# A Mamba block and a mixture-of-experts layer on one core: residual sums, layer-norm sums and Newton steps moved between engines

## The chip, the cores and the metric

One core of one Trainium2 chip. The time is the device time of one execution in microseconds (us); it is the median of three runs. The core has five engines that run their own instruction queues in order and meet through semaphores: TensorE (PE), VectorE (DVE), ScalarE (ACT), GpSimd (POOL) and SyncE (SP), which issues the transfers. A difference below about 0.2% can't be told from no change.

## The reference, cut to what matters

The input is 4 sequences of 2048 tokens with 256 features. With a state-space layer of 512 inner channels and 16 states, and a router that picks 2 of 4 experts (a shared matrix and a rank-4 addition for each):

```
x  = x + ssm(layernorm(x))
       u = W_in LN(x) + b_in -> x_i (512), z (512)
       dt, B, C = W_x x_i + b_x ;  delta = softplus(W_dt dt + b_dt)
       h_t = h_(t-1) * exp(delta_t A) + x_t * delta_t * B_t ;  y_t = sum over states of h_t C_t
       out = W_out ((y + D x_i) * silu(z)) + b_out
x  = x + moe(layernorm(x))
       logits = W_g LN(x) + b_g ; top 2 of softmax -> w
       out = sum over the 2 experts of w * W_o relu(W_i LN(x) + B_e A_e LN(x))
layernorm(x) = (x - mean) / sqrt(var + 1e-5)
```

## The kernel before, in words

**Tiles.** The 8192 tokens are cut into 16 chunks of 512. A chunk is 4 tiles of 128 tokens by 256 features where tokens lie on partitions (`xin`, `xr`, `x1`, 0.5 MB each), and tiles of 128 channels by 512 tokens where channels do. The scan works on 512 channels x 16 states = 64 units of 128 rows (32 channels x 4 states) by 512 tokens.

**Main loop.** A chunk has 16 steps (`s`), a step 4 units (`j`). For each step GpSimd multiplies delta*x by B for all four units into `hs` (L1344, `times_b`, one step ahead). For each unit ScalarE writes exp(delta A) into a PSUM bank, `decay` (L1089), and VectorE scans it with `hs` (L1286). Then the result is multiplied by C: the first two units of a step always by VectorE (L1276), the last two by GpSimd in 12 of the 16 steps (L1356, `POOL_STEPS`), by VectorE in the others. TensorE sums the products over the states into `y_ps` (L946). ScalarE keeps the last column of the scan as the next chunk's state (L1103, `keep_state`), and only then writes the next `decay` into the same bank.

**Side jobs.** All else is cut into jobs of a letter and a number, and tables of rows (`PE_SIDE`, `ACT_SIDE`, `DVE_SIDE`, `POOL_SIDE`, `SP_SIDE`) say at which step and which quarter of it an engine runs which job: a row is a step, `|` separates the four quarters (two for TensorE). "pre" is work for the next chunk, "main" for this one, "post" for the one before, "late" for the one before that. The jobs run in each engine's queue behind the scan work of that quarter. `LAST` and `END` are tables of their own for the last chunk and the tail after it. The jobs that matter here:
- N (`stats`): sums of the first layer norm on VectorE, `bn_stats` for 4 tiles (N0), `bn_aggr` for 4 (N1). P0 and P1 the same for the second norm.
- A1/A2 of POOL (`center`, L663 to L666): variance + eps, minus the mean, minus half the variance. R (L1039, L1041): 1/sqrt by Ln and Exp on ScalarE. O1/O2 of POOL (`newton`, L673 to L682): one Newton step on it, five instructions of 128x4. O and Q of ACT (L1047): the normalising itself.
- A, G: transposes; B, E: W_in; C: W_x, copied by ScalarE twice (L1001, L1002; the second rounds to fp32r), then VectorE subtracts it to keep the rest (L1167, `dt_st` of 64 rows). D: W_dt. L, M, U, V: softplus.
- Y of PE and F: W_out, whose result VectorE adds to `xr` (L1187, the first residual). H, I, X, M: the router. J, S, T: the experts' hidden layer; K: W_o, 8 products of 256 columns (L932), whose result VectorE adds to `x1` (L1190, the second residual). SyncE stores `x1`.
- W of POOL (L1330), a 128x4 product of the router's weights.

PSUM has eight banks: four of `decay`, one of `y_ps`, and three that the jobs share in the order of the PE table (`assign_banks`); a bank is free when the engine that evacuates it is done (`freed_at`).

Semaphores count finished instructions. `xin` of the next chunk is loaded when A1 has read it, `xr` when G1 has read it (step 11).

## Time and profile before

| | |
|---|---|
| median of 3 runs | 1964.43 us (1963.17 to 1964.9) |
| the profiled execution | 1968.13 us, of which the span 1966.3 us |
| busy share of the span | PE 83%, VectorE 93%, ScalarE 73%, GpSimd 91% |
| instructions | PE 6816, VectorE 2246, ScalarE 2755, GpSimd 780 |
| transfers | 234.92 MB, mean 119 GB/s |
| granted TensorE clock, mean | 0.933 of full |

The span runs from the first to the last instruction of the profile. Busy time is the time in which an engine had at least one instruction under way; records of neighbours overlap a little. A groups row has the line, the engine, the operation, output<-input with shapes and count, then the busy time and the mean ns of one, then the time in which the engine stood idle just before such an instruction and who ended it. GpSimd and VectorE are the busiest; the share of a whole span mixes prologue, 14 alike chunks and a tail.

### The profile page before, as it was taken

Reading aid. Unit: us, or ns where it says so; the run is one execution under the profiler, and the core shown is the slowest. Engines: PE = TensorE matmul, PEld = TensorE weight load, DVE = VectorE, ACT = ScalarE, POOL = GpSimd, SP = SyncE. Lnnn points to the kernel's source line nnn. Section 1 sums busy time; section 2 is a strip of 40 time slices with the busy share of each in tenths; the row PEclk is TensorE's granted clock in tenths of the full one; section 3 lists DMA queues with packets and bytes.
Section 4 is the critical chain, followed back from the end, with each engine's and each line's share of the span. In section 5 each row is a group of like instructions: output and inputs, shape, how many; then the busy total and the mean of one; then the engine's idle time right before and its main releaser. Section 6 shows DMA issues by size and latency. Waiting matters only on the chain.

```text
span 1966.3 us, 25727 instructions
## 1 busy us (share of the span) xinstructions
PE 1628.6 (83%) x6816; PEld 808.6 (41%) x6816; DVE 1823.1 (93%) x2246; ACT 1431.6 (73%) x2755; POOL 1791.7 (91%) x780
## 2 busy tenths in 40 slices
PE   3364779898898989889898988889898898988899
PEld 1111224444443444444344444444444444444456
DVE  2799999999999999999999999999999999999951
ACT  3566767877787777878777787877778787777643
POOL 1899999999999999999999999999999999999920
PEclk8666879999899999989999999999999999999999
DMA  4646553544646365464636536463643646265200
GB/s 167 142 112 155 119 138 90 142 123 92 161 111 155 91 152 123 96 151 112 161 84 149 126 92 152 112 165 79 158 118 94 148 111 166 68 156 118 58 14 19
DMA packets 146761, 234.92 MB, mean 119 GB/s; under 512 B 22064, under 2 KB 46896, under 8 KB 146096
## 3 DMA queue, kind: packets, MB, share of 16 engines
q1 hardware_dynamic: 146608, 233.18, 48.7%
q8 instruction: 59, 0.97, 0.2%
q14 instruction: 94, 0.77, 0.1%
HBM read 190.11 MB, written 42.99 MB: 119 GB/s over the span
## 4 chain that ended last, share of the span: by engine, by line
DVE 32%; POOL 23%; issue 17%; PE 17%; ACT 5%; DMA 1%; DVEq 0%; SPq 0%; POOLq 0%; ACTq 0%
POOL hs L1344 14%; DVE decay L1286 13%; DVE hs L1276 8%; DVE hs L1286 7%; POOL hs L1356 6%; PE bank L910 4%; PE bank L932 4%; ACT decay L1089 2%; PE y_ps L946 2%; POOL e_dt L1334 1%; DVE st L1146 1%; POOL z_dt L1323 1%; PE bank L894 1%; PE bank L914 1%; PE bank L884 1%
## 5 line engine op out<-in xcount | busy, mean ns | idle before, releaser
L1344 POOL TENSOR_TENSOR hs<-dx_rep,b_rep 128x2048 f32<-128x2048 f32 x256 | 1161.8, 4541 | 13.4 <-issue 11.1
L1286 DVE TENSOR_TENSOR_SCAN decay<-decay,state,hs 128x512 f32<-128x512 f32 x640 | 796.2, 1277 | 34.2 <-ACT decay L1089 27.4
L1089 ACT ACTIVATE decay<-dt_rep,a_sb 128x512 f32<-128x512 f32 x1024 | 690.0, 685 | 28.7 <-DMA dt_rep<-rep_scratch 10.3
L1286 DVE TENSOR_TENSOR_SCAN hs<-decay,state,hs 128x512 f32<-128x512 f32 x384 | 487.3, 1269 | 4.3 <-ACT decay L1089 3.7
L1356 POOL TENSOR_TENSOR hs<-hs,c_rep 128x1024 f32<-128x1024 f32 x192 | 453.6, 2362 | 6.3 <-ACT state L1103 6.3
L1276 DVE TENSOR_TENSOR hs<-decay,c_rep 128x1024 f32<-128x1024 f32 x320 | 385.1, 1204 | 0.0
L946 PE MATMUL y_ps<-hs,nsum 128*32 128x512 f32 x2048 | 290.3, 641 | 48.8 <-POOL hs L1356 30.6
L910 PE MATMUL bank<-w_i_sb,x_t 128*128 128x512 f32 x484 | 273.5, 693 | 28.9 <-DVE silu L1174 25.5
L868 PE MATMUL bank<-xn_t,w_in_sb 128*128 128x512 f32 x512 | 258.5, 635 | 14.5 <-ACT x_t L996 4.9
L1103 ACT COPY state<-decay 128x2 f32<-128x2 f32 x320 | 51.0, 159 | 266.8 <-DVE hs L1276 260.1
L932 PE MATMUL bank<-w_o_sb,r_t 128*128 128x256 f32 x944 | 224.1, 392 | 2.6 <-ACT r_t L1074 1.8
L932 PEld LDWEIGHTS bank<-w_o_sb,r_t 128*128 128x128 f32 x944 | 182.0, 195 | 50.4 <-ACT r_t L1074 15.7
L868 PEld LDWEIGHTS bank<-xn_t,w_in_sb 128*128 128x128 f32 x512 | 92.4, 197 | 141.4 <-issue 94.2
L910 PEld LDWEIGHTS bank<-w_i_sb,x_t 128*128 128x128 f32 x484 | 92.7, 209 | 136.0 <-issue 94.3
L927 PE MATMUL bank<-ident,r 128*128 128x128 f32 x928 | 123.4, 276 | 21.5 <-DVE x L1190 19.0
L927 PEld LDWEIGHTS bank<-ident,r 128*128 128x128 f32 x928 | 102.9, 140 | 61.5 <-DVE x L1190 30.2
L884 PE MATMUL bank<-w_out_sb,gated 128*128 128x256 f32 x496 | 121.1, 386 | 7.6 <-DVE x L1187 5.2
L1065 ACT ACTIVATE r<-bank,wgt 128x512 f32<-128x512 f32 x121 | 82.1, 679 | 45.3 <-PE bank L914 41.3
L884 PEld LDWEIGHTS bank<-w_out_sb,gated 128*128 128x128 f32 x496 | 90.3, 190 | 50.8 <-DVE x L1187 17.8
L946 PEld LDWEIGHTS y_ps<-hs,nsum 128*32 128x32 f32 x2048 | 42.2, 111 | 154.3 <-issue 139.6
L1069 ACT ACTIVATE r<-bank,wgt 128x512 f32<-128x512 f32 x121 | 81.9, 677 | 28.4 <-PE bank L839 28.2
L1334 POOL TENSOR_TENSOR e_dt<-e_dt,z_dt 128x1024 f32<-128x1024 f32 x32 | 75.5, 2358 | 27.6 <-ACT e_dt L1016 27.6
(163 smaller groups left out, 1747.7 us busy)
## 6 DMA issues: line engine op xcount, KB each, us to landing
dx_rep<-rep_scratch SPq DMA_DIRECT2D x256, 256.0 KB, 4.7
dt_rep<-rep_scratch SPq DMA_DIRECT2D x256, 256.0 KB, 7.6
b_rep<-bc_scratch SPq DMA_DIRECT2D x256, 64.0 KB, 3.9
rep_scratch<-z_dt SPq DMA_DIRECT2D x64, 256.0 KB, 2.5
rep_scratch<-e_dt SPq DMA_DIRECT2D x64, 256.0 KB, 2.7
c_rep<-bc_scratch SPq DMA_DIRECT2D x256, 64.0 KB, 2.6
xin<-in_u SPq DMA_DIRECT2D x16, 512.0 KB, 4.2
xr<-in_u SPq DMA_DIRECT2D x16, 512.0 KB, 4.3
```

Source lines behind the costliest of these rows:

```text
L868: mm = pe.matmul(ps[:], w_in_sb[:, k, col:col + P], xn_t[odd][:, k, :], start=k == 0, stop=k == KD - 1)
L884: pe.matmul(ps[:, cols], gated[odd][:, k, i * P:(i + 1) * P], w_out_sb[:, k, :], start=k == 0 and not (is_last(q) and i % 2), stop=False, ...
L910: pe.matmul(ps[:], x2_t[odd][:, k, t * P:(t + 1) * P], w_i_sb[:, k, cols], start=k == 0, stop=False, skip_group_check=is_last(q))
L927: mm = pe.matmul(ps[:, f * P:(f + 1) * P], r[i % 2][:, f * P:(f + 1) * P], ident[:], start=r is r1, stop=r is r2, is_transpose=True)
L932: mm = pe.matmul(ps[:, 0:D], r_t[:, f, :], w_o_sb[:, f, :], start=f == 0, stop=f == NF - 1)
L946: mm = pe.matmul(y_ps[32 * j:32 * j + 32, :], nsum[:], hs[s % 4][:, j, :], start=k == 0, stop=k == KG - 1, skip_group_check=True)
L1089: nc.scalar.activation(decay[:, j, :], dt_rep[m % 2][:, j, :], ACT.Exp, scale=a_sb[:, J * s + j:J * s + j + 1]).then_inc(decay_ready, 1)
L1276: v.tensor_tensor(hs[s % 4][:, js, :], decay[:, js, :], c_rep[:, k, :].unsqueeze(1).to_broadcast([P, 2, T]), ALU.mult).then_inc(prod_vecto ...
L1286: v.tensor_tensor_scan(hs[s % 4][:, j, :] if kept else decay[:, j, :], decay[:, j, :], hs[s % 4][:, j, :], state[:, b, n:n + 1], ALU.mult, ...
L1334: g.tensor_tensor(e_dt[:], e_dt[:], z_dt[:], ALU.add).then_inc(delta_ready, 1)
L1344: nc.gpsimd.tensor_tensor(hs[s % 4][:], dx_rep[m % 2][:], b_rep[:, k, :].unsqueeze(1).to_broadcast([P, J, T]), ALU.mult).then_inc(input_re ...
L1356: nc.gpsimd.tensor_tensor(hs[s % 4][:, 2:4, :], hs[s % 4][:, 2:4, :], c_rep[:, k, :].unsqueeze(1).to_broadcast([P, 2, T]), ALU.mult).then_ ...
```

## The change

The first residual: TensorE starts each F with a product identity x `xr`, and ScalarE copies the sum to `x1` with the row sums of its accumulator. The second residual: TensorE starts each K with identity x `x1`, ScalarE copies. The last chunk keeps VectorE's additions. The sums of both norms: ScalarE takes the row sums of x (N0, N1; or with the F copies), the mean (N2, P0), and the row sums of (x - mean)^2 by Square with the accumulator (N3, N4, P1, P2). The first chunk's first norm and the last chunk's second one keep `bn_stats` on VectorE (`FIRST`, `by_vector`). ScalarE also computes minus half the variance and the square of the root, so that Newton is three instructions, and these and the centering go to VectorE (O1 in step 1, O2 in step 7). The rest of dt: TensorE adds -identity x `dt_st` to C0's bank, ScalarE copies it (C1). The C product of step 14's last two units goes from GpSimd to VectorE. The tables have a new order of jobs.

```diff
 ACT_SIDE = [
+    "N0 pre, N1 pre | N2 pre | N3 pre | N4 pre, S1 late",
+    "R1 pre | J2 late | J3 late | T1 late, O0 pre, O1 pre, O2 pre",
...
+    "S4 late | E1 main | J5 late, V1 main, R2 post, W1 main, Z1 main | ",
+    "Q0 post | Q1 post, C0 pre | K1 late, C1 pre | D0 pre",
...
 DVE_SIDE = [
-    "N0 pre, N1 pre |  |  | ",
-    " |  |  | Y3 post",
...
+    "O1 pre |  |  | Y3 post",
...
+    " |  | O2 post, S1 main | ",
...
 POOL_SIDE = [
-    "A1 pre, O1 pre",
+    "",
...
-    "A2 post",
-    "O2 post",
+    "",
+    "",
...
-POOL_STEPS = [s for s in range(STEPS) if s % KG < 3]
+POOL_STEPS = [s for s in range(STEPS) if s % KG < 3 and s != 14]
...
+FIRST = dict(SIDE, act=[[[x for x in part if x[0] != "N"] for part in row] for row in SIDE["act"]],
+             dve=[[["N0 pre", "N1 pre", "A1 pre", "O1 pre"]] + [[]] * (J - 1)] +
+             [[[x for x in part if x != "O1 pre"] for part in row] for row in SIDE["dve"][1:]])
...
+        def newton(dve, i, q):
+
+            v = nc.vector
...
+            dve.wait_ge(halved, q + 1)
+            dve.wait_ge(root, 3 * (q + 1))
+            v.tensor_tensor(nw[:, 1], nw[:, 0], nw[:, 3], ALU.mult).then_inc(steps, 1)
+            dve.wait_ge(steps, NEWTON_STEPS * q + 1)
+            v.scalar_tensor_tensor(out=rs[:], in0=nw[:, 1], scalar=1.5, in1=rs[:], op0=ALU.add, op1=ALU.mult).then_inc(steps, 1)
+            dve.wait_ge(steps, NEWTON_STEPS * q + 2)
+            v.tensor_tensor(nt[:], nw[:, 4], rs[:], ALU.mult).then_inc(steps, 1)
...
+                if letter == "C" and i == 1:
...
+                    pe.wait_ge(dt_hi, q + 1)
+                    pe.matmul(banks[used("C0", c, AHEAD[when])[0]][:], neg_id[:], dt_st[:], start=False, stop=True,
+                              skip_group_check=True).then_inc(dt_rest, 1)
+                    return
...
                 elif letter in "YF":
...
+                    if not is_last(q):
+                        if i == 0:
+                            pe.wait_ge(xr_loaded, 16 * (q + 1))
+                        pe.matmul(ps[:, cols], ident[:], xr[:, i, :], start=True, stop=False)
...
                 elif letter == "K":
+                    if not is_last(q):
+                        needs("F", i)
+                        pe.matmul(ps[:, 0:D], ident[:], x1[odd][:, i, :], start=True, stop=False)
...
+                elif letter == "N":
+                    if i == 0:
+                        act.wait_ge(xin_loaded, 16 * (q + 1))
+                    if i < 2:
+                        for t in (2 * i, 2 * i + 1):
+                            last = nc.scalar.activation(xin[:, t, :], xin[:, t, :], ACT.Identity, accum_out=sum1[:, t:t + 1])
+                        last.then_inc(ln1_sum, 1)
+                    elif i == 2:
+                        act.wait_ge(ln1_sum, 2 * q)
+                        nc.scalar.mul(nw1[:, 4], sum1[:], -1.0 / D).then_inc(ln1_mean, 1)
+                    else:
+                        if i == 3:
+                            act.wait_ge(ln1_mean, q)
+                        for t in (2 * i - 6, 2 * i - 5):
+                            last = nc.scalar.activation(xn_t[odd][:, t // 2, t % 2 * D:t % 2 * D + D], xin[:, t, :], ACT.Square, bias=nw1[:, 4, t:t + 1],
+                                                        accum_out=sq1[:, t:t + 1])
+                        last.then_inc(ln1_var, 1)
+                elif letter == "F":
+
+                    at_least(act, out_stored[i], 16 * (q - 1))
+                    ps, free = wait_filled(act, job[:2], c, when)
+                    nc.scalar.activation(x1[odd][:, i, :], ps[:, 0:D], ACT.Identity, accum_out=sum2[:, i:i + 1]).then_inc(free, 1)
...
+                elif letter == "K":
+                    ps, free = wait_filled(act, job[:2], c, when)
+                    nc.scalar.copy(x1[odd][:, i, :], ps[:, 0:D]).then_inc(free, 1)
...
                 elif letter == "R":
...
+                        nc.scalar.activation(nw[:, 3], sq[:], ACT.Identity, scale=-0.5 / D,
+                                             bias=consts[:, 4, 0:1]).then_inc(halved, 1)
+                        nc.scalar.activation(rs[:], sq[:], ACT.Ln, scale=1.0 / D, bias=consts[:, 0, 0:1]).then_inc(root, 1)
...
                     nc.scalar.activation(rs[:], rs[:], ACT.Exp, scale=-0.5).then_inc(root, 1)
+                    act.wait_ge(root, 3 * q + 2)
+                    nc.scalar.activation(nw[:, 0], rs[:], ACT.Square).then_inc(root, 1)
```

## Rows read from the trace of the kernel before

**Rows 1.** Busy time in one stretch: columns PE, PEld, DVE, ACT, POOL, granted clock, DMA.

```profile
200.00:1800.00 1600.00, 1385.11 (x5866) 685.95 (x5865) 1575.24 (x1919) 1239.57 (x2388) 1567.17 (x679) 0.95 0.52 124
```

**Rows 2.** Groups of VectorE instructions, 200 to 1800 us: busy, mean ns, idle before.

```profile
L1286 DVE TENSOR_TENSOR_SCAN decay<-decay,state,hs 128x512 f32<-128x512 f32 x559 | 695.8, 1277 | 8.5 <-ACT decay L1089 5.1 <-POOL hs L1344 0.6 <-issue 0.2
L1286 DVE TENSOR_TENSOR_SCAN hs<-decay,state,hs 128x512 f32<-128x512 f32 x336 | 426.5, 1269 | 4.2 <-ACT decay L1089 3.7
L1276 DVE TENSOR_TENSOR hs<-decay,c_rep 128x1024 f32<-128x1024 f32 x280 | 337.0, 1204 | 0.0
...
L1190 DVE TENSOR_TENSOR x<-bank,x 128x256 f32<-128x256 f32 x53 | 22.0, 416 | 6.4 <-PE bank L932 6.4
...
L1146 DVE BATCH_NORM_STATS2 st<-xin 128x6 f32<-128x256 f32 x52 | 18.1, 412 | 0.0
L1167 DVE SCALAR_TENSOR_TENSOR dt_st<-bank,b_x_sb,dt_st 64x512 fp32r<-64x512 f32 x14 | 10.6, 757 | 0.5
L1151 DVE BATCH_NORM_AGGREGATE mv<-st 128x2 f32<-128x6 f32 x108 | 10.2, 158 | 2.4 <-DVE st L1146 2.4
```

**Rows 3.** Timeline of GpSimd within one chunk: start us, us, instruction, idle before.

```profile
744.72 0.24 POOL L663 TENSOR_TENSOR ve<-mv,consts 128x4 f32<-128x4 f32 x1
...
747.29 4.55 POOL L1344 TENSOR_TENSOR hs<-dx_rep,b_rep 128x2048 f32<-128x2048 f32 x1
751.80 2.37 POOL L1356 TENSOR_TENSOR hs<-hs,c_rep 128x1024 f32<-128x1024 f32 x1
754.11 4.56 POOL L1344 TENSOR_TENSOR hs<-dx_rep,b_rep 128x2048 f32<-128x2048 f32 x1
...
790.50 0.20 POOL L663 TENSOR_TENSOR ve<-mv,consts 128x4 f32<-128x4 f32 x1
...
790.96 4.54 POOL L1344 TENSOR_TENSOR hs<-dx_rep,b_rep 128x2048 f32<-128x2048 f32 x1
...
797.79 0.19 POOL L673 TENSOR_TENSOR nw<-rs 128x4 f32<-128x4 f32 x1
...
799.05 4.54 POOL L1344 TENSOR_TENSOR hs<-dx_rep,b_rep 128x2048 f32<-128x2048 f32 x1
```

**Rows 4.** The same groups view for GpSimd, 200 to 1800 us.

```profile
L673 POOL TENSOR_TENSOR nw<-rs 128x4 f32<-128x4 f32 x27 | 5.4, 201 | 20.6 <-ACT rs L1041 20.6
```

**Rows 5.** Timeline of VectorE: a product; the last chunk's Newton steps.

```profile
757.64 1.20 DVE L1276 TENSOR_TENSOR hs<-decay,c_rep 128x1024 f32<-128x1024 f32 x1
758.75 1.27 DVE L1286 TENSOR_TENSOR_SCAN hs<-decay,state,hs 128x512 f32<-128x512 f32 x1
...
1904.76 0.16 DVE L673 TENSOR_TENSOR nw<-rs 128x4 f32<-128x4 f32 x1 [0.31 <-ACT rs L1041]
1904.96 0.16 DVE L676 TENSOR_TENSOR nw<-nw 128x4 f32<-128x4 f32 x1
```

**Rows 6.** Timeline of the prologue, VectorE and GpSimd, 9 to 14 us.

```profile
10.59 1.38 DVE L1120 TENSOR_TENSOR w_dt_st<-hs,w_dt_st 32x512 fp32r<-32x512 f32 x2
...
11.50 0.53 POOL L676 TENSOR_TENSOR nw<-nw 128x4 f32<-128x4 f32 x1
...
12.11 0.20 POOL L678 TENSOR_TENSOR nw<-nw,consts 128x4 f32<-128x4 f32 x1
```

**Rows 7.** Durations min/median/max of two lines over the whole run.

```profile
L676 POOL TENSOR_TENSOR nw<-nw x31: 198/201/531, 11.5 to 1820.9; 128x4 f32<-128x4 f32 x31
...
L1127 DVE TENSOR_SCALAR skip<-ident,d_sb x4: 274/274/306, 12.1 to 12.7; 128x128 f32<-128x128 f32 x4
```

**Rows 8.** Groups of ScalarE instructions, 200 to 1800 us.

```profile
L1074 ACT COPY r_t<-bank 128x512 f32<-128x512 f32 x107 | 61.7, 576 | 21.3 <-PE bank L927 21.3
L1103 ACT COPY state<-decay 128x2 f32<-128x2 f32 x279 | 44.5, 160 | 215.0 <-DVE hs L1276 208.5 <-issue 5.2
...
L1047 ACT ACTIVATE xr<-x,nt,rs 128x256 f32<-128x256 f32 x56 | 31.7, 589 | 2.8 <-POOL nt L682 2.8
```

**Rows 9.** Timeline of TensorE: the eight products of one K job.

```profile
823.18 3.62 PE L932 MATMUL bank<-w_o_sb,r_t 128*128 128x256 f32 x16
```

More of the change, by code:

```diff
@@ L151 @@
 PE_LAST = [
-    "T0 late, S1 late | J2 late",
-    " | T1 late, E0 main",
+    "S1 late | J2 late",
+    "T1 late | E0 main",
     "S2 late, F0 post, J3 late | K0 late",
-    "S3 late | T2 late, F1 post",
-    "F2 post | ",
-    "F3 post, T3 late, E1 main, J4 late | S4 late",
-    "K1 late, T4 late | ",
+    "S3 late | F1 post",
+    "F2 post, T2 late, F3 post | ",
+    "T3 late | J4 late, E1 main",
+    "K1 late, S4 late, T4 late | ",
     "J5 late | S5 late, T5 late",
-    "E2 main | ",
+    " | E2 main",
     "G0 post | ",
@@ L163 @@
     "J7 late | S7 late, T6 late, T7 late",
-    "K3 late | I0 post",
-    "E3 main, J0 post | S0 post, J1 post, T0 post",
-    "S1 post | T1 post, J2 post, K0 post",
+    "E3 main, K3 late, I0 post | ",
+    "J0 post | S0 post, J1 post",
+    "T0 post, S1 post | T1 post, J2 post, K0 post",
     " | S2 post",
@@ L376, in tables @@
         return LAST if c == NC - 1 else END
-    return SIDE
+    return FIRST if isinstance(c, int) and c < 0 else SIDE
 def parts_of(c):
@@ L403, in bank_jobs @@
                     name = {"Y": "F", "Z": "J"}.get(name[0], name[0]) + name[1]
-                if name[0] in BANK_JOBS:
+                if name[0] in BANK_JOBS and name != "C1":
                     yield name, when, J * s + j
@@ L410, in freed_at @@
     letter = name[0]
-    if letter in "FKC":
-        engine, by = "dve", name
+    if letter in "FK":
+        engine, by = "dve" if c == NC and when == "post" else "act", name
+    elif letter == "C":
+        engine, by = "act", "C1"
     elif letter == "E":
@@ L593, in block_program @@
         weights_ready = sem("weights_ready")
-        NEWTON_STEPS = 5
+        ln1_sum, ln1_mean, ln2_mean, dt_rest = (sem(n) for n in ("ln1_sum", "ln1_mean", "ln2_mean", "dt_rest"))
+        NEWTON_STEPS = 3
         def vector_products(c, s, h):
@@ L996, in job_act @@
                     nc.scalar.activation(x_t[odd][:, i, :], ps[:], ACT.Identity, bias=b_in_sb[:, i:i + 1]).then_inc(free, 1)
+                elif letter == "N":
[19 more added lines that the diff above has]
+                    nc.scalar.activation(x1[odd][:, i, :], ps[:, 0:D], ACT.Identity, accum_out=sum2[:, i:i + 1]).then_inc(free, 1)
+                elif letter == "P":
+                    if i == 0:
+                        wait_read(act, c, when, "F", range(TT))
+                        nc.scalar.mul(nw2[:, 4], sum2[:], -1.0 / D).then_inc(ln2_mean, 1)
+                    else:
+                        if i == 1:
+                            act.wait_ge(ln2_mean, q + 1)
+                        for t in (2 * i - 2, 2 * i - 1):
+                            last = nc.scalar.activation(xr[:, t, :], x1[odd][:, t, :], ACT.Square, bias=nw2[:, 4, t:t + 1],
+                                                        accum_out=sq2[:, t:t + 1])
+                        last.then_inc(ln2_var, 1)
+                elif letter == "K":
+                    ps, free = wait_filled(act, job[:2], c, when)
+                    nc.scalar.copy(x1[odd][:, i, :], ps[:, 0:D]).then_inc(free, 1)
+                elif letter == "C" and i == 1:
+                    act.wait_ge(dt_rest, q + 1)
+                    b, _ = used("C0", c, AHEAD[when])
+                    nc.scalar.activation(dt_st[64:128], banks[b][64:128], ACT.Identity,
+                                         bias=b_x_sb[64:128, 0:1]).then_inc(freed[b], 1)
@@ L1111, in _ @@
             v.memset(state[:], 0.0)
-            for n, value in enumerate((EPS, -0.5, 1.5, -1.0)):
+            for n, value in enumerate((EPS, -0.5, 1.5, -1.0, -0.5 * EPS)):
                 v.memset(consts[:, n], value)
@@ L1140, in split_lora, with stats @@
                 last.then_inc(weights_split, 1)
-            def stats(i, q, src, st, mv, part):
+            def stats(i, src, st, mv, part):
                 if i == 0:
@@ L1147, in stats @@
                 else:
-                    dve.wait_ge(part, 2 * q + 1)
+                    dve.wait_ge(part, 1)
                     dve.sem_inc(dve_turn, 1)
```

87 lines of the change are left out of this document (39 added, 48 removed), and 134 rows, old and new, of tables (ACT_END, ACT_LAST, ACT_SIDE, DVE_END).

## The prediction, made before the changed kernel was run

> **What bounds the kernel now.** I read the page first: its busy shares name VectorE (93%) and GpSimd (91%) together, which settles nothing between them. So next the busy time of a stretch without prologue and tail, 200 to 1800 us [rows 1]. The groups view of that stretch counts 559 + 336 = 895 scans [rows 2]; a chunk has 64, so 1600 us hold 13.98 chunks and a chunk takes 114.4 us. Per chunk VectorE is busy 1575.24/13.98 = 112.7 us, GpSimd 112.1, TensorE 99.1, ScalarE 88.7 [rows 1]. Two engines are within 2 us of the period, and they feed each other (GpSimd fills hs for the scan and multiplies what the scan leaves), so relieving one alone gives nothing. ScalarE spends 208.5 us of the stretch waiting in its state copies for VectorE's product [rows 8], 14.9 us a chunk: it is a follower with slack. VectorE waits for ScalarE's decay for only 5.1 + 3.7 us, 0.6 a chunk [rows 2].
>
> A record overlaps the next one: the product at 757.64 lasts 1.20 and the scan behind it starts 1.11 later [rows 5]. I price an instruction by that slot, its duration less 0.08 to 0.09.
>
> **The change, part by part, per chunk.**
>
> VectorE loses:
> - four F and four K additions (the F form is the K form with another operand): 8 x (0.416 - 0.085) = 2.6 [rows 2];
> - both layer norms' statistics: 8 x (0.412 - 0.085) = 2.6, and eight aggregations 8 x (0.158 - 0.08) = 0.6 with 2.4/13.98 = 0.2 of wait [rows 2], together 3.4;
> - the rest of dt, 0.757 - 0.08 = 0.7 [rows 2], which becomes a product with -identity on TensorE and a copy on ScalarE.
> It gains one more C product, 1.1 [rows 5], since step 14 leaves GpSimd, and two Newtons of three dependent instructions. The last chunk does such steps on VectorE already, one every 0.20 us [rows 5]: 2 x 3 x 0.20 = 1.2. Net 6.7 - 2.3 = 4.4 less; 112.7 becomes 108.3.
>
> GpSimd loses one C product, 754.11 - 751.80 = 2.3, the centering and Newton of the first norm with the wait for the root inside it, 747.29 - 744.72 = 2.6, and those of the second, (790.96 - 790.50) + (799.05 - 797.79) = 1.7 [rows 3]. That is 6.6, of which 20.6/13.98 = 1.5 was wait and not busy [rows 4]: its busy time goes to 112.1 - 5.1 = 107.0. It is now beside VectorE's 108.3 and slightly under it, so VectorE sets the period.
>
> ScalarE gains 20 instructions of 256 columns (N 8, F 4, P 4, K 4). The trace has none without pointer operands; a 256-column one with two of them takes 0.589 and a 512-column copy 0.576 [rows 8], so a slot of about 0.49 is the upper end and half of the copy, 0.24, the lower. I take 0.33, nearer to the copy since most have one pointer operand or none: 6.6. The second dt copy costs at most a copy's 0.5 to 0.6, the two means, two halves and two squares of 128x4 about 0.2 each (they are of the size of the state copy, 0.160 [rows 8]): 1.2. Sixteen of them also write an accumulator, which no row shows: from nothing to another small instruction of 0.2 each, so 0 to 3.2; I take 1.6. Sum 10.0 (6.5 to 15); ScalarE goes from 88.7 to 98.7. At nothing this is hidden by the 14.9 us in which it waits for VectorE; but the cover is thinner: the period shrinks too, and the exponential of a step can only be written after VectorE's product has read the bank, with one scan (1.277 - 0.085 = 1.19 [rows 2]) of room before the next one is wanted. Steps 0 (N0, N1 in the first quarter, N3, N4 and S1 behind), 1 (the root, then the Newton that VectorE waits for) and 7 (J5, V1, the root, W1, Z1 in one quarter, all ahead of the next exponential, with O2 waiting in the middle on VectorE) have about no room left. Today VectorE is idle 114.4 - 112.7 = 1.7 a chunk; I take 2.5 after, between 1.7 (nothing added) and 5 (each of the three steps late by a 1.2 us scan).
>
> TensorE gains eight fp32 products of 256 columns, the amount of one K job, 3.6 [rows 9], and the -identity product, under 1: 99.1 becomes 103.6. What waits behind it is mainly ScalarE's evacuations; its clock is at 0.95 of full in the stretch, mostly the higher level (2.4 GHz) [rows 1], and more work can't be expected to lower it. If the cover failed, each microsecond would appear as VectorE's wait for a gated or silu input; I leave it inside the 2.5.
>
> The dt chain gets longer: copy, product, copy, then D0 instead of copy, subtraction, D0. Its result is wanted by GpSimd three steps, some 20 us, later; no cost. K, written by ScalarE instead of VectorE, still precedes its store in the queue; the store's place on SP does not move, and F needs xr three steps after its load. No cost. Prologue and tail keep their statistics and their additions of the last chunk on VectorE; plus or minus 2 us.
>
> Sum: period 108.3 + 2.5 = 110.8 against 114.4, 3.6 a chunk. Fifteen chunks run these tables; the chunk before the tail has no first norm and gains about half. 15.5 x 3.6 = 56. The profiled execution took 1968.1 (span 1966.3), 3.7 above the median of 1964.4; off the median that gives 1909, for which I say 1910. Own range 1893 to 1940 (VectorE's idle time between 1.5 and 4.7).
>
> **Rival A, the other side: VectorE's Newton steps are held by GpSimd.** All three take both tensors from SBUF. In the prologue VectorE runs two such instructions from 10.59 to 11.97; GpSimd's L676 starts inside them at 11.50 and takes 0.53, to 12.03, that is until VectorE is done [rows 6], while the median of its 31 is 0.201 [rows 7]. So one engine holds the other. The reverse shows only in small: the longest of four skip instructions (0.306 against 0.274) has the 128x4 GpSimd instruction of 12.11 beside it [rows 6, 7]. In the steady stretch no two-SBUF VectorE instruction meets a long GpSimd one: the scan and the product read decay from PSUM, the statistics have one input. The Newtons would, 30 times (15 first norms, 15 second ones). If VectorE must wait for the instruction that GpSimd is in, the first step waits on average (16 x 4.54^2 + 15 x 2.36^2)/(2 x 108) = 1.9 us, the second, coming 0.20 after the first, for the whole next one, mean 3.5, and the third for up to as much, unless GpSimd has by then run out of scans: 5.4 to 8.9, say 6. Behind a held step stand the next scan and the C product in VectorE's queue, and ScalarE's state copy, the next exponential and GpSimd's product wait for those, so all of it is period: 30 x 6 = 180, time 1910 + 180 = 2090 (2060 to 2150). It decides from 56/30 = 1.9 a Newton: one single wait each (A1) already returns the whole gain, 1966. Against it: only the small case is shown, and a 128x4 instruction may slip in where a long one could not.
>
> The Trainium skill (SBUF — State Buffer, Who interferes with whom) says that a VectorE instruction with two SBUF inputs contends with a GpSimd instruction that reads SBUF, and that the one that starts first keeps the shared ports for its whole length. By that rule the time is that of rival A, not the 1910. The trace agrees for one direction with its 0.53 against 0.20 us [rows 6, 7]; no long GpSimd instruction here shows the other.
>
> **Rival B: ScalarE becomes the bound.** If the accumulator costs a good deal more than a small instruction (0.5 each, 8 a chunk), ScalarE stands at 105 plus its hand-overs, and VectorE waits 4 to 6 a chunk instead of 2.5. For it: steps 0, 1 and 7. Against: nothing in the trace has a ScalarE instruction that costs more than its columns and operands. Period 112.3 to 113.8, time 1930 to 1955, say 1945.
>
> **Chances.** Forecast 0.47, rival A 0.36, A1 0.07, B 0.10. Less than 0.2% (4 us) can't be told from no change. Faster: 0.47 + 0.06 (most of B) + 0.02 (half of A1's lower side) = 0.55; same: 0.05; slower: 0.36 + 0.04 = 0.40. The likeliest is 1910; because rival A holds a third, the range must reach into it: 1893 to 2110.
>
> **What would show it.** In the changed kernel's groups view the three Newton lines on VectorE at 0.16 each, with under 0.5 idle ahead, speak for 1910; durations of microseconds in them, or a GpSimd instruction lengthened beside them, for rival A. VectorE's wait for decay should grow from 0.6 to 1 or 2 us a chunk; if it grows to 4, B. ScalarE's accumulating 256-column instructions should start 0.25 to 0.6 apart, its waits in the state copies should fall from 14.9 to about 5, TensorE should be busy about 103 to 104 a chunk, and GpSimd should show waits of 3 a chunk where it shows none now. The forecast is wrong if VectorE's busy time per chunk is not within 1 us of 108.3, or if its idle time is above 5.

## Result and the profile after: 7% slower

The changed kernel takes 2101.9 us (median of four runs, 2097.6 to 2104.9) against 1964.2 before in the same job: ratio 1.070, 95% interval 1.0676 to 1.0723. The forecast, 1910, has the wrong sign; rival A, 2090, is 12 us off.

First the busy time of the same stretch in the changed kernel, which answers to [rows 1] (columns PE, PEld, DVE, ACT, POOL, clock):

```profile
200.00:1800.00 1600.00, 1393.20 (x5672) 723.40 (x5671) 1499.55 (x1563) 1273.36 (x2780) 1394.57 (x418) 0.91 0.48 116
```

and the groups of VectorE, which answer to [rows 2]; the last three are the steps of Newton:

```profile
L1357 DVE TENSOR_TENSOR_SCAN decay<-decay,state,hs 128x512 f32<-128x512 f32 x549 | 685.4, 1277 | 48.7 <-ACT decay L1166 47.5 <-POOL hs L1412 0.3 <-issue 0.2
L1357 DVE TENSOR_TENSOR_SCAN hs<-decay,state,hs 128x512 f32<-128x512 f32 x286 | 363.2, 1270 | 23.5 <-ACT decay L1166 23.4
...
L697 DVE TENSOR_TENSOR nt<-nw,rs 128x4 f32<-128x4 f32 x26 | 59.5, 2290 | 0.9
L695 DVE SCALAR_TENSOR_TENSOR rs<-nw,rs 128x4 f32<-128x4 f32 x26 | 31.2, 1202 | 0.9
...
L693 DVE TENSOR_TENSOR nw<-nw 128x4 f32<-128x4 f32 x26 | 4.9, 188 | 1.5 <-ACT nw L1118 0.8
```

549 + 286 = 835 scans are 13.05 chunks in 1600 us: a period of 122.6 us, where it was 114.4. Per chunk VectorE is busy 1499.55/13.05 = 114.9 us (forecast 108.3) and idle 7.7 (forecast 2.5); GpSimd is busy 106.9, ScalarE 97.6, TensorE 106.8. A last Newton step took 2.29 us on average; the same form in the last chunk of the kernel before took 0.16 [rows 5]. Three queues side by side in one chunk, changed kernel, VectorE, then GpSimd, then ScalarE:

```profile
720.25 0.16 DVE L693 TENSOR_TENSOR nw<-nw 128x4 f32<-128x4 f32 x1
720.44 2.23 DVE L695 SCALAR_TENSOR_TENSOR rs<-nw,rs 128x4 f32<-128x4 f32 x1
722.71 4.42 DVE L697 TENSOR_TENSOR nt<-nw,rs 128x4 f32<-128x4 f32 x1
727.05 0.74 DVE L1245 SCALAR_TENSOR_TENSOR silu<-bank,b_in_sb,e_gate 128x512 f32<-128x512 f32 x1
```
```profile
715.80 4.54 POOL L1412 TENSOR_TENSOR hs<-dx_rep,b_rep 128x2048 f32<-128x2048 f32 x1 [0.18 <-PE y_ps L973]
720.30 2.35 POOL L1424 TENSOR_TENSOR hs<-hs,c_rep 128x1024 f32<-128x1024 f32 x1
722.62 4.48 POOL L1412 TENSOR_TENSOR hs<-dx_rep,b_rep 128x2048 f32<-128x2048 f32 x1
```
```profile
727.16 0.60 ACT L1124 ACTIVATE xr<-x,nt,rs 128x256 f32<-128x256 f32 x1 [4.44 <-DVE nt L697]
```

The first step starts at 720.25, just before GpSimd's instruction of 720.30, and takes 0.16. The second starts 0.14 us after that instruction and ends, at 722.67, when it ends (722.65). The third ends at 727.13, with the next GpSimd instruction (727.10). Meanwhile ScalarE stands 4.44 us in the normalizing instruction for the shift nt, with the next exponentials behind it. Every chunk of the stretch has this at its second norm (6.8 to 7.6 us for the three steps). The first norm's steps, in the same chunk, fall where GpSimd stands still:

```profile
674.64 0.15 DVE L693 TENSOR_TENSOR nw<-nw 128x4 f32<-128x4 f32 x1
...
675.03 0.16 DVE L697 TENSOR_TENSOR nt<-nw,rs 128x4 f32<-128x4 f32 x1
```
```profile
664.75 9.02 POOL L1412 TENSOR_TENSOR hs<-dx_rep,b_rep 128x2048 f32<-128x2048 f32 x2
675.63 2.37 POOL L1424 TENSOR_TENSOR hs<-hs,c_rep 128x1024 f32<-128x1024 f32 x1 [1.86 <-ACT state L1180]
```

Over the whole run the three lines are busy 132.1 us in 96 instructions; at 0.16 each they would be 15.4. So VectorE is held for 117 us: 6.3 us at the second norm of each steady chunk, 7 in each of the first norms at 66 and 180 us, 12.5 in the Newton at 1943 us, none in the other first norms. That is most of the 138 us lost, but it is not yet the 192 us between forecast and result.

### The profile page after: what moved, and what is told of

Its sections match the earlier page's. It is cut to its first block, busy times and chain, and to the rows that moved or that the text cites. A ratio compares the mean times of both kernels' runs of the same rounds, so it can differ in the third digit from the quotient of the medians.

```text
span 2101.6 us, 26197 instructions
## 1 busy us (share of the span) xinstructions
PE 1745.9 (83%) x7072; PEld 903.8 (43%) x7072; DVE 1878.6 (89%) x1982; ACT 1573.4 (75%) x3403; POOL 1714.9 (82%) x516
## 4 chain that ended last, share of the span: by engine, by line
PE 45%; DVE 20%; ACT 13%; issue 12%; POOL 7%; DMA 1%; SPq 0%; DVEq 0%; ACTq 0%; POOLq 0%
DVE decay L1357 8%; PE bank L891 7%; PE bank L934 7%; PE bank L959 7%; PE y_ps L973 6%; DVE hs L1347 5%; POOL hs L1412 5%; PE bank L908 4%; ACT decay L1166 4%; DVE hs L1357 3%; PE bank L918 2%; PE bank L938 1%; PE bank L862 1%; DVE rs L695 1%; PE bank L951 1%
## 5 line engine op out<-in xcount | busy, mean ns | idle before, releaser
L1357 DVE TENSOR_TENSOR_SCAN decay<-decay,state,hs 128x512 f32<-128x512 f32 x672 | 838.3, 1277 | 87.3 <-ACT decay L1166 85.1
L1424 POOL TENSOR_TENSOR hs<-hs,c_rep 128x1024 f32<-128x1024 f32 x176 | 417.0, 2369 | 72.8 <-DVE decay L1357 39.8
L1357 DVE TENSOR_TENSOR_SCAN hs<-decay,state,hs 128x512 f32<-128x512 f32 x352 | 446.9, 1270 | 25.8 <-ACT decay L1166 25.7
L1347 DVE TENSOR_TENSOR hs<-decay,c_rep 128x1024 f32<-128x1024 f32 x336 | 403.9, 1202 | 0.0
L973 PE MATMUL y_ps<-hs,nsum 128*32 128x512 f32 x2048 | 304.8, 671 | 31.0 <-POOL hs L1424 22.5
L934 PE MATMUL bank<-w_i_sb,x_t 128*128 128x512 f32 x480 | 268.4, 687 | 19.9 <-ACT low_t L1135 12.5
L959 PE MATMUL bank<-w_o_sb,r_t 128*128 128x256 f32 x944 | 243.4, 417 | 0.9 <-ACT r_t L1151 0.9
L959 PEld LDWEIGHTS bank<-w_o_sb,r_t 128*128 128x128 f32 x944 | 202.5, 215 | 35.9 <-issue 1.1
L862 PE MATMUL bank<-lora_st,low_t 64*128 64x512 f32 x120 | 67.6, 563 | 43.1 <-ACT r L1142 43.1
```

The costliest lines, as they stand in the source:

```text
L862: pe.matmul(banks[used(f"J{i}", c, AHEAD[when])[0]][:], low_t[64:128, t * P:(t + 1) * P], lora_st[64:128, half * 512:(half + 1) * 512], st ...
L934: pe.matmul(ps[:], x2_t[odd][:, k, t * P:(t + 1) * P], w_i_sb[:, k, cols], start=k == 0, stop=False, skip_group_check=is_last(q))
L959: mm = pe.matmul(ps[:, 0:D], r_t[:, f, :], w_o_sb[:, f, :], start=f == 0 and is_last(q), stop=f == NF - 1)
L973: mm = pe.matmul(y_ps[32 * j:32 * j + 32, :], nsum[:], hs[s % 4][:, j, :], start=k == 0, stop=k == KG - 1, skip_group_check=True)
L1347: v.tensor_tensor(hs[s % 4][:, js, :], decay[:, js, :], c_rep[:, k, :].unsqueeze(1).to_broadcast([P, 2, T]), ALU.mult).then_inc(prod_vecto ...
L1357: v.tensor_tensor_scan(hs[s % 4][:, j, :] if kept else decay[:, j, :], decay[:, j, :], hs[s % 4][:, j, :], state[:, b, n:n + 1], ALU.mult, ...
```

## Experiments

All ratios are to the kernel before, timed in the same job, with 95% intervals. They come in four groups.

### Is it the second SBUF input that holds Newton?

**e1, Newton on GpSimd.** The changed kernel with Newton where it was, in four instructions.

```diff
-    "O1 pre |  |  | Y3 post",          # VectorE's table, step 1
-    " |  | O2 post, S1 main | ",       # step 7
+    "O1 pre",                          # GpSimd's table, step 1
+    "O2 post",                         # step 7
```

> [...] Port theory: VectorE's period of 122.6 us a chunk holds 6.7 us of held Newton steps and, behind them, most of the 6 us of idle time that came with them (ScalarE stands 4.6 us a chunk in the second norm's first normalising and is late with its exponentials); without them 110.5 to 112 a chunk, 1910 to 1935 us in all. Load theory (ScalarE's 9 us and TensorE's 4 us more a chunk cause the idle time, the holds only fill part of it): the idle time stays, 2102 - 16 x 6.7 = 1995 or more. Chain theory (GpSimd now waits for the root inside its own queue and passes that on): GpSimd idle before the first step above 3 us a chunk and a time above 1960.

Measured 1982.8; 1.008 (1.0062 to 1.0097). 119 us come back, the 117 us of the held instructions and no more than that. But the time is 73 us above the forecast, so the first of the three expectations above is missed by 48 us. The third does not explain it: GpSimd shows no wait for the root ahead of these steps. **e2, the second norm's Newton alone on GpSimd:**

```diff
-    "O1 pre",                          # e1: GpSimd, step 1
+    "O1 pre |  |  | Y3 post",          # VectorE, step 1
```

> Only the second norm's Newton goes to GpSimd; the first norm's three steps stay on VectorE in step 1. Port theory: in the changed kernel the first norm's steps take 0.15 to 0.17 us each in all steady chunks, since GpSimd is idle there, so this should equal e1 within 0.5%, unless the new phase between the engines brings them onto a GpSimd instruction: then they are held too, up to 7 us a chunk, and the time is 1990 to 2020. Load theory: as e1, 1995 or more.

Measured 1994.0; 1.014 (1.0118 to 1.0162): the second norm is 108 of the 119 us, the first 11. These 11 are not lost in the steady chunks, where the first norm's three steps take 0.47 us together, but in two early ones: at 65 and 179 us they take 7.7 us each.

**e3, one SBUF input.** The same three places and dependences, on VectorE:

```diff
-            v.tensor_tensor(nw[:, 1], nw[:, 0], nw[:, 3], ALU.mult).then_inc(steps, 1)
+            v.tensor_reduce(nw[:, 1], nw[:, 0].unsqueeze(2), AX, ALU.add).then_inc(steps, 1)
...
-            v.tensor_tensor(nt[:], nw[:, 4], rs[:], ALU.mult).then_inc(steps, 1)
+            v.tensor_reduce(nt[:], nw[:, 4].unsqueeze(2), AX, ALU.add).then_inc(steps, 1)
```

> The changed kernel with the three Newton instructions on VectorE at the same place with the same waits, but as reductions over an axis of one element: one SBUF input each instead of two (first norm of chunk 0 and second norm of chunk 15 keep theirs). Leaves out the Newton refinement and the scaling of the shift by the root. Port theory: none of the three is held whatever GpSimd does (0.15 to 0.17 each), 1905 to 1930 us. If the steps wait for semaphores or for the order of the queues and not for GpSimd's instruction, it stays at 2102.

Measured 1982.3; 1.0081 (1.0064 to 1.0098). Its timeline, VectorE and then GpSimd, shows two steps that start inside a GpSimd instruction and take 0.16; so do the second and the third step in 16 of 28 Newtons, and none of these reductions takes longer:

```profile
340.31 0.16 DVE L701 TENSOR_REDUCE nw<-nw 128x4 f32<-128x4 f32 x1
340.51 0.16 DVE L706 TENSOR_REDUCE nt<-nw 128x4 f32<-128x4 f32 x1
```
```profile
340.18 2.35 POOL L1435 TENSOR_TENSOR hs<-hs,c_rep 128x1024 f32<-128x1024 f32 x1
```

**e10, pointer scalars.** Each step as four instructions of one column, whose second operand is a pointer scalar:

```diff
-            v.tensor_tensor(nt[:], nw[:, 4], rs[:], ALU.mult).then_inc(steps, 1)
+            for t in range(TT):
+                last = v.tensor_scalar(nt[:, t:t + 1], nw[:, 4, t:t + 1], rs[:, t:t + 1], None, ALU.mult)
+            last.then_inc(steps, 1)
```

> The changed kernel, complete, with Newton on VectorE at the same place but each step as four instructions of 128x1 with one tensor from SBUF and the other factor as a scalar by pointer, instead of one with two tensors. If only a second tensor takes the port, none is held and the time is e1's and e3's, 1975 to 1990 us. If a scalar by pointer from SBUF takes it too, the twelve are held like the three: 2100 us or more.

Measured 1979.8; 1.0071 (1.0052 to 1.009). VectorE in one chunk, and GpSimd beside it:

```profile
680.76 0.58 DVE L694 TENSOR_SCALAR nw<-nw 128x1 f32<-128x1 f32 x4 [0.16 <-ACT nw L1124]
...
681.99 0.58 DVE L702 TENSOR_SCALAR nt<-nw,rs 128x1 f32<-128x1 f32 x4
```
```profile
680.81 2.35 POOL L1430 TENSOR_TENSOR hs<-hs,c_rep 128x1024 f32<-128x1024 f32 x1
```

Not held: a second operand given as a pointer escapes what a second tensor does not. None of the run's 384 such instructions took more than 0.22 us.

Both e3 and e10 also change the kind of instruction. That it isn't the kind shows in the changed kernel itself: the router has a TENSOR_TENSOR of the same 128x4, with one input in a PSUM bank. It starts inside a long GpSimd instruction 15 of 16 times and never takes more than 0.17 us; VectorE, then GpSimd:

```profile
764.70 0.16 DVE L1323 TENSOR_TENSOR lm<-bank,mx 128x4 f32<-128x4 f32 x1
```
```profile
762.56 4.55 POOL L1412 TENSOR_TENSOR hs<-dx_rep,b_rep 128x2048 f32<-128x2048 f32 x1
```

**e4, the kernel before with nothing changed but Newton's engine**, five steps on VectorE:

```diff
-    "A1 pre, O1 pre",                  # GpSimd, step 0
+    "O1 pre |  |  | Y3 post",          # VectorE, step 1
-    "O2 post",                         # GpSimd, step 7
+    " |  | S1 main | O2 post",         # VectorE, step 7
```

> The kernel before with one part of the change alone: the Newton steps (five each) on VectorE, O1 in step 1, O2 at the end of step 7; centering stays on GpSimd, nothing else moves. Port theory: GpSimd is idle under 2 us a chunk, so most steps meet one of its instructions: 6 to 12 us a Newton, GpSimd relieved of 2.5 us a chunk, 30 Newtons: 2110 to 2250 us. Without a port: GpSimd is relieved and VectorE has 2 us a chunk more: 1960 to 1995 us.

Measured 2176.0; 1.1078 (1.1056 to 1.1099). Its groups, and one chunk (VectorE, then GpSimd):

```profile
L676 DVE TENSOR_TENSOR nw<-nw 128x4 f32<-128x4 f32 x25 | 59.6, 2384 | 0.9
L678 DVE TENSOR_TENSOR nw<-nw,consts 128x4 f32<-128x4 f32 x25 | 59.4, 2375 | 0.9
L673 DVE TENSOR_TENSOR nw<-rs 128x4 f32<-128x4 f32 x25 | 28.9, 1157 | 0.0
```
```profile
742.89 4.43 DVE L676 TENSOR_TENSOR nw<-nw 128x4 f32<-128x4 f32 x1
747.36 4.42 DVE L678 TENSOR_TENSOR nw<-nw,consts 128x4 f32<-128x4 f32 x1
```
```profile
742.80 8.95 POOL L1344 TENSOR_TENSOR hs<-dx_rep,b_rep 128x2048 f32<-128x2048 f32 x2
```

211 us for 30 Newtons, 7.0 each; the held time alone, (59.6 + 59.4 + 28.9)/25 less 0.5, is 5.4. Rival A's 6 a Newton is near this mean, but no single Newton is: the second norm's is held 9.4 us and the first norm's about 1.2. The last two of the five steps are never held, and of the first norm's only the first step is: while VectorE is held GpSimd runs out of scanned data and stands. The changed kernel pays less (117/30 = 3.9): one short and one long GpSimd instruction at the second norm, and nothing at most first norms. The hold is settled: it comes with two tensors from SBUF and goes when one of them is left out, is a pointer scalar or lies in PSUM.

### Where are the other 73 us? ScalarE's load, or TensorE's products

e1's stretch answers to the forecast's sum without the held steps (columns as above):

```profile
200.00:1800.00 1600.00, 1439.76 (x5998) 743.15 (x5997) 1490.71 (x1575) 1347.26 (x2930) 1497.36 (x550) 0.92 0.52 124
```

Its period, from one gated product to the same one of the next chunk, is 115.6 us in the mean of 14: VectorE busy 107.7, idle 7.9, ScalarE busy 97.3, TensorE 104.0, GpSimd 108.2. All the loads are the forecast's (GpSimd's with Newton put back); only the idle time is not. (Counted by its 881 scans, as the kernel before was, the period is 116.2 us, VectorE busy 108.3 and idle 7.9.) Its waits (total, times, longest):

```profile
DVE decay L1362 <- ACT decay L1171: 42.1, 72, 5.2
DVE lg L1295 <- PE bank L923: 23.5, 12, 2.4
DVE hs L1362 <- ACT decay L1171: 22.0, 40, 1.2
DVE silu L1250 <- ACT e_gate L1109: 16.4, 13, 1.3
```

**e5, light ScalarE:** e1 with the passes of both norms on 8 columns and without accumulators, **e6, no identity:** e1 without the eight identity products, and **e7**, both.

```diff
-  last = nc.scalar.activation(xin[:, t, :], xin[:, t, :], ACT.Identity, accum_out=sum1[:, t:t + 1])
+  last = nc.scalar.activation(xin[:, t, 0:8], xin[:, t, 0:8], ACT.Identity)     # e5, N; P alike
-  pe.matmul(ps[:, cols], ident[:], xr[:, i, :], start=True, stop=False)         # e6, F
-  pe.matmul(ps[:, 0:D], ident[:], x1[odd][:, i, :], start=True, stop=False)     # e6, K
```

> e1 (Newton on GpSimd) with less time on ScalarE and the same instructions, order and waits: no accumulator outputs (16 reads of 0.09 slot each, 1.5 us a chunk) and the twelve sum and square instructions of N and P on 8 columns instead of 256 (12 x 0.21 = 2.5 us). Leaves out most of the layer norms' sums. If VectorE's 7 us of idle time a chunk come from ScalarE's load, they fall by most of these 4.0 us: 1983 - 15.5 x (2.5 to 4) = 1921 to 1944 us. If they come from TensorE being late with what ScalarE and VectorE evacuate, 1975 to 1983 us.

> e1 without the eight identity products a chunk on TensorE (3.6 us); all waits stay. Leaves out both residuals outside the last chunk. ScalarE theory: 1975 to 1983 us. TensorE theory: VectorE's idle time falls by 2 to 3.6 us a chunk: 1927 to 1952 us.

> e5 and e6 together. If one of the two engines alone is the cause, equal to the better of e5 and e6; if each covers for the other (both must have room), clearly lower than both, down to VectorE's busy 108.2 + 1.7 a chunk: 1895 to 1910 us.

Measured e5 1990.5, 1.0111 (1.0085 to 1.0136); e6 1952.3, 0.9937 (0.9898 to 0.9976); e7 1957.8, 0.9948 (0.9929 to 0.9967). e5's ScalarE is busy 1298.04 us in the stretch instead of 1347.26, and VectorE is busy as before (1490.41): 3.6 us a chunk off ScalarE's load gives nothing back. Rival B falls although its sign, the wait for decay (4.6 a chunk in e1), is there. The products cost about 30 us; TensorE's 3.6 us a chunk would be 56 at full price. The 30 is rough: e6's ten runs lie between 1945 and 1978 us, and the four above 1969 had a granted clock of 0.90 to 0.91, the others 0.93. e7 is not below e6, so neither engine covers for the other. Since e6 leaves the residuals out, it is no candidate.

**e8, e1 with the second residual back on VectorE:**

```diff
-    "K0 late, F0 post |  | M1 main, F1 post | ",    # ScalarE, step 3; K1, K2, K3 alike
+    "K0 late |  |  | ",                             # VectorE, step 3
```

> e1 with the second residual as in the kernel before: TensorE without identity products in K, VectorE adds K to x1 (+1.3 us busy a chunk), ScalarE without the four copies (-1.1 us), TensorE -1.8 us. A complete kernel. With the idle time caused by ScalarE's or TensorE's load, about even: idle time down 1.3 to 2.5, busy up 1.3: 1965 to 1985 us. If neither, VectorE's 1.3 add to it: 2003 us.

Measured 1984.8; 1.0086 (1.0062 to 1.0109): no difference to e1.

### Is it the order of the jobs?

**e9**: e1 with F1 to F3, S1 and H0 to H2 a quarter step later, **e11**: e10 with the same moves, **e12**: e9 with 12 of 16 C pairs on GpSimd.

```diff
-    " |  | H0 post | H1 post, S2 main, H2 post",       # VectorE, steps 10 and 11
-    "H3 post | H4 post | H5 post | H6 post",
+    " |  |  | S2 main, H0 post",
+    "H1 post, H2 post, H3 post | H4 post | H5 post | H6 post",
```

> e1 (Newton on GpSimd) with five jobs later in the same queues: on VectorE the route's H0, H1, H2 one quarter of a step and S1 one quarter; on ScalarE F1, F2, F3 one quarter. In e1 VectorE waits 1.7 us a chunk for TensorE at H0, 1.2 for ScalarE at S1, and ScalarE about 2 at the F copies with its exponentials behind them. Order theory (the engines have room, the orders are too early): 1.7 + 1.2 + up to 2 of the 7.4 us of idle time go: 1983 - 15.5 x (3 to 4.5) = 1913 to 1937 us. Saturation theory (TensorE is behind in the middle of the chunk and whoever waits, waits for it): the waits reappear behind, 1965 to 1983 us.

> e10 with the five jobs of e9 later. Order theory: as e9, 1915 to 1940 us, and the best complete kernel, since GpSimd has no Newton. Saturation theory: 1965 to 1983 us. If pointers are held: e10 less at most 60 us.

> e9 with 12 of 16 C pairs on GpSimd as in the kernel before: VectorE 1.1 us a chunk less, GpSimd 2.3 more (111 busy). If VectorE's busy time still sets the period: 15 us below e9. If TensorE or ScalarE set it, equal to e9 within 5 us; if GpSimd does, above.

Measured e9 2028.3, 1.0319 (1.0296 to 1.0341); e11 2025.1, 1.0301 (1.0279 to 1.0322); e12 2030.0, 1.0318 (1.0295 to 1.0341). Against e1 and e10 that is a loss of 45 us. The waits for the router's bank and for e_gate did go, but VectorE's waits for decay rose, in e9 from the 42.1 of e1 to this:

```profile
DVE decay L1362 <- ACT decay L1171: 95.2, 93, 3.7
```

TensorE waits longer too. Once a chunk it stands, up to 7.9 us, until VectorE's router instruction `pk` is done, 26.2 us in all in e9 as in e11 (3.8 in e1, 4.1 in e10), and at another bank until VectorE's silu is done, 25.6 and 21.7 us (0.9 and 1.6). Which of the five moves costs the 45 us was not tried. In e12 VectorE's busy time is 0.7 us a chunk less than in e9 and the time is the same. The waits that were moved out of one queue came back in another, and larger.

### The residual and the sums, each by itself

**e13**: the kernel before with the eight identity products, overwritten by the projection behind them. **e16**: the kernel before with the residual part alone, its copies on ScalarE at the places where VectorE had added.

```diff
+  pe.matmul(ps[:, cols], ident[:], xr[:, i, :], start=True, stop=True)          # e13; stop=False in e16
+  nc.scalar.copy(x1[odd][:, i, :], ps[:, 0:D]).then_inc(free, 1)                # e16, ScalarE, F and K
```

**e14**: the reverse, e8 with the first residual on VectorE too, no identity products, the second norm's sums by a pass over x1. **e15**: e14 with 12 of 16 pairs.

```diff
-  nc.scalar.activation(x1[odd][:, i, :], ps[:, 0:D], ACT.Identity, accum_out=sum2[:, i:i + 1]).then_inc(free, 1)
+  nc.scalar.activation(xr[:, i, :], x1[odd][:, i, :], ACT.Identity, accum_out=sum2[:, i:i + 1]).then_inc(ln2_sum, 1)
```

> The kernel before with eight identity products of 256 columns a chunk that the projection behind them overwrites: TensorE gains 3.6 us a chunk, nothing else moves. If the products cost by TensorE's load (the 30 us that leaving them out of the changed kernel gave back), the time rises by 15 to 40 us, to 1980 to 2005, and VectorE's waits for a bank grow. If they only cost beside the additions' move to ScalarE, TensorE's 99.1 of 114.4 us has room and the time stays within 6 us of before.

> The residual part of the change alone: the kernel before, its eight additions a chunk as identity products on TensorE and copies on ScalarE, statistics and Newton on GpSimd as before. VectorE loses 2.6 us a chunk, ScalarE gains 2.6, TensorE 3.6. GpSimd keeps its 112.1, so no theory expects a large gain: hidden work, 1955 to 1968. If the products' load is what costs, it stands with the run that has the products alone; if it is ScalarE's queue standing at banks that TensorE fills late, it stands 10 to 30 us above that run.

> The change without its residual part: Newton on GpSimd, both residuals added by VectorE as before, the sums of the second norm by a pass of ScalarE over x1, sums of the first norm, squares, the rest of dt and 11 of 16 pairs as in the changed kernel. VectorE is busy 109 + 2.6 = about 111 a chunk, GpSimd about 108, TensorE 100. If the products cause the missing gain, the idle time of VectorE falls to 3 to 4 us and the time is 1940 to 1960, at or under the run without identity products (1952); if the idle time comes from the ScalarE chains of the norms, it stays at 7 and the time is 2010 to 2020.

> The same with 12 of 16 pairs of C products on GpSimd, as before the change: VectorE about 110, GpSimd about 110.5. If the idle time is a fixed cost of the hand-overs, the time is lower than with 11 by up to 15 us; if GpSimd with its Newton steps is the bound, it is higher by 10 to 30 us.

Measured e13 1975.2, 1.0045 (1.0031 to 1.006); e16 2031.5, 1.0316 (1.0282 to 1.035); e14 1989.7, 1.0128 (1.0111 to 1.0145); e15 1993.9, 1.0146 (1.0129 to 1.0163). The products alone cost 9 us, less than the 15 to 40 that a cost by TensorE's load was to give. e14 lies between its two expectations and decides neither; e15 is no faster than e14, so one C product more or less on VectorE doesn't matter there. The additions' move to ScalarE costs 56 more, where 10 to 30 was expected, though it takes 2.6 us a chunk off VectorE. The waits of e16 say how:

```profile
ACT x L1012 <- PE bank L941: 91.6, 37, 4.8
...
DVE decay L1302 <- ACT decay L1105: 58.3, 68, 2.1
...
DVE hs L1302 <- ACT decay L1105: 31.1, 19, 3.6
```

ScalarE stands 91.6 us for the bank of the second residual, at most 4.8 at a time, nearly four scans; the exponential stands behind it, and VectorE's wait for decay goes from 8.8 [rows 2] to 89.4 us. The changed kernel has another table: in e1 the copies of the second residual wait 14.5 us and those of the first 29.2. That fits with e8, which found nothing left to gain there.

e14 settles that the sums alone do not pay either. Its period is 115.6, as e1's, with VectorE busy 109.8 and idle 5.8 where the kernel before has 1.7. One chunk of it shows a wait that went through three engines (VectorE, TensorE, ScalarE, VectorE):

```profile
737.10 0.43 DVE L1255 TENSOR_TENSOR x<-bank,x 128x256 f32<-128x256 f32 x1
```
```profile
737.59 3.78 PE L935 MATMUL bank<-w_i_sb,x_t 128*128 128x512 f32 x4 [2.10 <-DVE x L1255]
```
```profile
742.13 0.69 ACT L1136 ACTIVATE r<-bank,wgt 128x512 f32<-128x512 f32 x1 [2.24 <-PE bank L939]
```
```profile
743.63 1.29 DVE L1351 TENSOR_TENSOR_SCAN decay<-decay,state,hs 128x512 f32<-128x512 f32 x1 [1.41 <-ACT decay L1160]
```

**e17, the second norm's root behind the gate's chain, e18, two more moves** (first norm's normalizing instructions later, K3 earlier):

```diff
-    "S4 late | E1 main | J5 late, V1 main, R2 post, W1 main, Z1 main | ",   # ScalarE, steps 7, 8
-    "Q0 post | Q1 post, C0 pre | C1 pre | D0 pre",
+    "S4 late | E1 main | J5 late, V1 main, W1 main, Z1 main | R2 post",     # e17
+    " | Q0 post, C0 pre | Q1 post, C1 pre | D0 pre",
-    "S3 main |  | K3 late | ",                                              # VectorE, step 14
+    "S3 main | K3 late |  | ",                                              # e18
```

> The kernel with the sums on ScalarE alone (1989.7), with one thing moved in ScalarE's order of step 7: the four instructions of the second norm's root behind the gate's logarithm and exponential (as in the kernel before) and the first two normalizing instructions a quarter later for that. If a wait that a chain of ScalarE instructions causes is lost time of its own, VectorE's 1.17 us a chunk for e_gate goes and nothing takes its place: 15 x 1.2 = 18 us less, about 1972. If the idle time only moves (the normalized rows come later, VectorE then waits longer for the router's bank), the time stays at 1985 to 1995.

> The same, and two moves more: the first norm's normalizing instructions a quarter later (ScalarE stood 1.05 us a chunk for GpSimd's shift there, VectorE 0.94 for the exponential behind it), and the last second residual of a chunk a quarter earlier on VectorE (TensorE stood 2.1 us for it at 735.5, its next product took 3.78 instead of 1.98 us, ScalarE stood 2.24 and VectorE 1.41 us). If each of these is lost time of its own, another 0.9 + 1.4 us a chunk goes: 1972 - 35 = about 1937, under the kernel before. If the chain through the banks sets the pace, it stays within 10 us of the run with the one move.

Measured e17 2000.3, 1.0183 (1.0166 to 1.02); e18 1975.4, 1.0061 (1.0042 to 1.008). In e17's waits the place that was mended and the one that took over stand side by side; e14 had 16.5 and 13.9 us there:

```profile
DVE lg L1284 <- PE bank L919: 24.6, 13, 2.6
...
DVE silu L1239 <- ACT e_gate L1098: 7.3, 13, 0.6
```

9 us of waiting gone at the gate, 11 more at the router. Less waiting at one place was outweighed: e17 is about 10 us slower than e14, where 1972 or 1985 to 1995 was expected. The other two moves do help, by 25 us, where 35 were hoped for: e18 has a period of 114.5 (the kernel before, counted in the same way, 114.0) and the best time of the versions that leave nothing out, still 11 us over the kernel before. None of them beats it.

## Why the prediction was wrong

**The step that failed first** is the price of VectorE's Newton steps: "It gains ... two Newtons of three dependent instructions. The last chunk does such steps on VectorE already, one every 0.20 us ...: 2 x 3 x 0.20 = 1.2." In the last chunk GpSimd runs nothing beside them. In the steady stretch the three lines took (59.5 + 31.2 + 4.9)/13.05 = 7.3 us a chunk, and 117 us in the whole run were hold. e1, e3 and e10 take it away in three different ways and all land within 3 us of each other, 119 to 122 us lower. Rival A described this with the right mechanism and nearly the right time, but at 0.36 it stood behind the forecast. The evidence was the 0.53 against 0.20 us of [rows 6, 7]: it showed that VectorE can hold GpSimd. It was discounted as "only the small case", though nothing in the trace spoke against the large one. Of A's own terms, the wait of the first step came out smaller (0.16 in the steady chunks, where it starts 0.05 us before GpSimd's next instruction), the second and third as said (2.2 and 4.4 us, a whole GpSimd instruction each), and the first norm of a steady chunk goes free. Its sum came near partly because it stood on a base of 1910 that is wrong too: 1910 + 180 against a real 1983 + 119. That it came within 12 us is luck in its size, not in its mechanism.

By the Trainium skill (SBUF — State Buffer, Who interferes with whom) a VectorE instruction with at most one SBUF input, outside the modes that use both ports for one tensor, does not contend with GpSimd; one with two contends with a GpSimd instruction that reads SBUF. The runs agree, e3 with 0.16 us inside a GpSimd instruction and the changed kernel with 2.23 and 4.42.

**The second step that failed** is the idle time: "I take 2.5 after, between 1.7 (nothing added) and 5". Without held steps the idle time is 7.9 us a chunk (e1), 7.1 in e3 (1502.11 busy in 1600 us, period 115.5). At 15.5 chunks, 5.4 us more idle less 0.6 us less busy is 74 us, the gap of 73 between 1910 and 1983. About 30 us of it hang on the identity products (e6), where the forecast had said that TensorE's work is hidden; alone in the kernel before they cost 9 (e13). ScalarE's load, the forecast's own worry, is not the cause: 3.6 us a chunk less of it gave nothing back (e5). What is left, 42 us above 1910 even in e6, no run isolates. The waits point to the longer chain of the norms through ScalarE, in single places of about 1 us each that partly give way when moved (e18, -25) and partly come back elsewhere (e17, e9), but that is argued, not shown. Nor was the clock separated from it: the forecast said that more work on TensorE can't be expected to lower its 0.95, and in the same stretch it was 0.91 in the changed kernel, 0.92 in e1 and 0.94 in e6, but 0.96 in e13, which adds TensorE's work alone.

**Steps that held.** VectorE without holds 107.7 and 108.4 a chunk (108.3 forecast). ScalarE 97.6 (98.7): the groups' means are 0.400, 0.493, 0.379, 0.498 and 0.368 us for the five kinds of 256-column instructions, four of each a chunk; 8.6 less about 0.1 of overlap each is 6.6, as forecast. TensorE 104.0 in e1 (103.6), though 106.8 in the changed kernel, at its lower clock. GpSimd 106.9 (107.0). ScalarE's wait in the state copies fell to 78.9/13.05 = 6.0 (about 5 forecast). The accumulator, which no row had shown, is an instruction of its own; ScalarE in e14:

```profile
666.37 0.42 ACT L1043 ACTIVATE xr<-x 128x256 f32<-128x256 f32 x1 [0.63 <-DVE x L1252]
666.69 0.19 ACT L1043 ACTIVATION_READ_ACCUMULATOR xr<-x 128x1 f32 x1
666.78 0.68 ACT L1160 ACTIVATE decay<-dt_rep,a_sb 128x512 f32<-128x512 f32 x1
```

It lasts 0.19 us but the next starts 0.09 later: 16 x 0.09 = 1.5 a chunk (1.6 taken). That is far from the 0.5 each that rival B needed. So without the holds each engine's load was forecast to within about 1 us, and the time was still 192 us off: both failures lie in what happens between engines.

Two ranges don't follow from their own terms, which changes nothing above: an idle time of 4.7 gives 1943, not 1940, and rival A's 5.4 to 8.9 a Newton gives 2072 to 2177, not 2060 to 2150.

## What to carry to other kernels

Before small work moves to VectorE beside a GpSimd that is never idle, count the SBUF tensors of each instruction: with two, each dependent step can cost the whole instruction that GpSimd is in, so count up to GpSimd's instruction length times the number of steps, until GpSimd runs out of work that VectorE feeds it, and everything queued behind. If it must be there, give the second operand as a pointer scalar (e10) or read it from PSUM (the router's 0.16 us). Where two engines are near the period and idle only 1 to 2 us of it, taking work off one was worth nothing here, because it added hand-overs to the queue that feeds both; the instruction that is moved should be judged by what stands behind it while it waits (e16: 2.6 us a chunk taken off VectorE, 56 us lost beside those of the products), not by its length.
